# Int8 fake-quantisation in two passes over the data instead of three

## The reference

```python
def _qdq(x):
    s = jnp.maximum(jnp.max(jnp.abs(x), axis=-1, keepdims=True) / 127.0, 1e-08)
    return jnp.clip(jnp.round(x / s), -127.0, 127.0) * s

def _L1_xattn_ref(x, cond, wq, bq, wkv, bkv, wp, bp):     # x: layernorm of the residual
    q = _qdq(x) @ _qdq(wq).T + bq
    kv = cond @ wkv.T + bkv
    ...
    attn = jax.nn.softmax(jnp.einsum('bnhd,bmhd->bhnm', q, k) * scale, axis=-1)   # 16 heads of 16
    o = jnp.einsum('bhnm,bmhd->bnhd', attn, v).reshape(B, N, C)
    out = _qdq(o) @ _qdq(wp).T + bp
    return out
```

## Time and profile before

| | |
|---|---|
| Time, median of 3 executions | 794.25 us (792.49 to 796.47) |
| The profiled execution, its own time | 794.42 us |
| Its span in the profile | 792.6 us |
| TensorE matmul busy | 638.2 us, 81% of the span |
| VectorE busy | 490.2 us, 62% |
| ScalarE busy | 314.7 us, 40% |
| GpSimd busy | 241.4 us, 30% |

### The profile page before, as it was taken

One profiled execution on the slowest core, in us unless ns is written; L12 is line 12 of the kernel. 1 busy time (PEld: TensorE's weight loads), 2 busy tenths in 40 slices (PEclk: granted clock), 3 DMA queues, 4 the chain that ended last, 5 costly groups with the idle time before them and its releaser, 6 DMA issues.

```text
span 792.6 us, 11112 instructions
## 1 busy us (share of the span) xinstructions
PE 638.2 (81%) x3798; PEld 399.0 (50%) x3799; DVE 490.2 (62%) x1022; ACT 314.7 (40%) x534; POOL 241.4 (30%) x247
## 2 busy tenths in 40 slices
PE   1651879986973299999786998887999999999990
PEld 1241525544662135556444666554666666666660
DVE  6998588875988899898666777963222222222223
ACT  4910423324567038887653666502111111111110
POOL 3312055547821199740322312002111111111100
PEclk9675879998996559999987999979999999999996
DMA  7000402010004434651306004970000000000005
GB/s 266 0 0 15 158 0 68 14 54 1 1 1 98 107 91 104 183 152 60 103 7 279 1 1 168 412 310 27 24 24 27 26 26 26 26 22 25 20 15 172
DMA packets 32318, 61.72 MB, mean 78 GB/s; under 512 B 6232, under 2 KB 26712, under 8 KB 29944
## 3 DMA queue, kind: packets, MB, share of 16 engines
q1 hardware_dynamic: 24480, 48.93, 19.3%
q10 hardware_dynamic: 5632, 6.29, 2.2%
q0 software_dynamic: 2160, 5.90, 2.2%
HBM read 47.22 MB, written 13.50 MB: 77 GB/s over the span
## 4 chain that ended last, share of the span: by engine, by line
PE 54%; DVE 32%; issue 6%; POOL 3%; ACT 3%; DMA 2%; SPq 0%; DVEq 0%; POOLq 0%; ACTq 0%
PE bank L1907 18%; PE bank L1928 8%; PE bank L1485 4%; DVE region L1213 3%; PE bank L1126 2%; PE bank L1086 2%; PE bank L1918 2%; DVE XN L366 2%; PE bank L542 2%; PE bank L1110 2%; PE bank L570 2%; PE bank L1505 2%; PE bank L506 2%; DVE region L2217 2%; POOL rstd L380 1%
## 5 line engine op out<-in xcount | busy, mean ns | idle before, releaser
L1907 PE MATMUL bank<-region,wide 128*128 x368 | 142.3, 540 | 1.6 <-issue 1.6
L1786 DVE TENSOR_TENSOR wide<-wide,bank 128x448 f32<-128x448 f32 x46 | 28.5, 621 | 120.0 <-ACT wide L1834 120.0
L1907 PEld LDWEIGHTS bank<-region,wide 128*128 128x128 f32 x368 | 68.1, 190 | 61.7 <-issue 61.5
L1213 DVE TENSOR_REDUCE region<-bank 128x2 f32<-128x512 f32 x128 | 80.1, 680 | 6.9 <-PE bank L1086 6.3
L1684 POOL DMA_INDIRECT choice_results<-wide,to_row x23 | 22.7, 987 | 182.9 <-DVE wide L1799 182.9
L1928 PE MATMUL bank<-region,XN 128*128 x322 | 73.4, 379 | 1.2 <-DVE wide L1799 1.2
L1149 ACT ACTIVATE region<-bank 128x1024 f32<-128x1024 f32 x64 | 62.9, 1024 | 15.6 <-PE bank L1110 15.5
L1834 ACT ACTIVATE wide<-bank 128x448 f32<-128x448 f32 x46 | 24.9, 543 | 106.2 <-PE bank L1907 106.2
L1928 PEld LDWEIGHTS bank<-region,XN 128*128 128x128 f32 x322 | 59.5, 190 | 9.3 <-issue 2.2
L1086 PE MATMUL bank<-region 128*128 128x256 bf16 x256 | 51.9, 304 | 8.8 <-DVE region L1213 6.0
L380 POOL TENSOR_TENSOR rstd<-vareps,half_neg 128x4 f32<-128x4 f32 x16 | 18.3, 1146 | 122.0 <-DVE vareps L376 122.0
(11 more groups left out here) (309 smaller groups left out, 1236.0 us busy)
## 6 DMA issues: line engine op xcount, KB each, us to landing
region<-in_L_ffn_experts_dram SPq DMA_DIRECT2D x8, 2688.0 KB, 15.9
region<-ctx_parts SPq DMA_DIRECT2D x24, 192.0 KB
region<-norm_parts SPq DMA_DIRECT2D x24, 192.0 KB
channel_values<-wide ACTq DMA_DIRECT2D x8, 512.0 KB, 3.8
ctx_parts<-region SPq DMA_DIRECT2D x40, 64.0 KB, 2.0
region<-in_L_ffn_w_gate_up_dram SPq DMA_DIRECT2D x4, 512.0 KB, 6.1
wide<-channel_values SPq DMA_DIRECT2D x16, 128.0 KB, 2.5
norm_parts<-region SPq DMA_DIRECT2D x24, 64.0 KB, 3.6
```

The costliest lines, as they stand in the source:

```text
L1213: e.tensor_reduce(nmax[i % 2][:, at_:at_ + KC], score_bank("scores", n).rearrange("p (c n) -> p c n", c=KC), AX.X, ALU.max, negate=True).t ...
L1786: e.tensor_tensor(HB8[par][:, cols], silu8[:, cols], bank[hf][:, 512:512 + I8 // 2], ALU.mult)\
L1907: last = e.matmul(bank[hf][:, 512 * gu:512 * gu + hw], xbT[par][:, P * c:P * c + P], region[:, bass.ds(off + (2 * gu + c) * I8 + hw * hf, ...
```

## The change

In each of the three places the minimum with 127 and the maximum with -127 are dropped. The first pass now multiplies by the reciprocal and adds `MAGIC`; the second pass is gone; the third is as it was. Nothing is moved, and no wait is added.

```diff
         def quantise(e, ch, src, dst, sc):
...
-            ch.link(e.tensor_scalar(dst, src, sc[:, 2:3], 127.0, ALU.mult, ALU.min))
-            ch.link(e.tensor_scalar(dst, dst, -127.0, MAGIC, ALU.max, ALU.add))
+            ch.link(e.tensor_scalar(dst, src, sc[:, 2:3], MAGIC, ALU.mult, ALU.add))
             return e.tensor_scalar(dst, dst, MAGIC, sc[:, 1:2], ALU.subtract, ALU.mult)
 
         def quantise_in_psum(e, ch, src, dst, sc):
...
-            ch.link(e.tensor_scalar(src, src, sc[:, 2:3], 127.0, ALU.mult, ALU.min))
-            ch.link(e.tensor_scalar(src, src, -127.0, MAGIC, ALU.max, ALU.add))
+            ch.link(e.tensor_scalar(src, src, sc[:, 2:3], MAGIC, ALU.mult, ALU.add))
             return e.tensor_scalar(dst.rearrange("p (h d) -> p h d", d=HD), src, MAGIC, sc[:, 1:2], ALU.subtract, ALU.mult)
...
                 for i in range(lo, hi):
                     xi = XN[:, D * i:D * i + D]
-                    last = e.tensor_scalar(xi, xi, inv[:, i - lo:i - lo + 1], 127.0, ALU.mult, ALU.min)
+                    last = e.tensor_scalar(xi, xi, inv[:, i - lo:i - lo + 1], MAGIC, ALU.mult, ALU.add)
                 ch.link(last)
-                ch.link(e.tensor_scalar(half, half, -127.0, MAGIC, ALU.max, ALU.add))
```

## The result

The changed kernel takes **788.47 us** in the median of 6 runs (787.08 to 790.22). The kernel before took 793.69 us in the median of 6 (792.13 to 796.47). The ratio is 0.9938, with a 95% interval from 0.992 to 0.9955: 5 us less, between 3.6 and 6.3. Forecast were 789.0 us.

The account below looks back on a forecast made before the run. VectorE was taken to bound the edited stretches, except where it waits for TensorE. 1.33 + 1.46 + 0.1 + 1.88 + 0.47 = 5.24 us off the 794.25 us median gave 789.0 us, range 786.5 to 792.3.

Parts of the forecast that it names:

- the likeliest case: Whole kernel: the forecast itself, 5.24 us gained, 789.0 us, own range 787.5 to 790.8, chance 0.62.
- The cost of one pass: Removed VectorE passes, start to start: 0.33 us (weights), 0.73 (normalised input), 0.47 (PSUM); surviving first steps stay at 354 and 494 ns.
- cheaper first steps: All 20 surviving first passes: if as cheap as the two-constant form, another 1.2 us would go; kept for the range.
- Weights, 1.33: Four weight pieces: each removal counts in full in VectorE's stream, 0.33 us each, 1.33 us together.
- Normalised input, 1.46: Two halves of the normalised input: both removals count in full, 0.73 us each, 1.46 us together.
- the cover: TensorE's transposes after the first half: they waited 0.99 us for L729, so their own work ends before its new end.
- The loop, 0.1 + 1.88 + 0 + 0.47: Attention loop, eight tiles: first gives 0.1 us, tiles 1 to 4 give 1.88, 5 and 6 nothing, 7 gives 0.47.
- All the signs: Loop: L769 every 4.91 us, L570 waiting about 0.17, first L769 about 0.4, L786 waits grown to 1.4 and 1.9.
- The rival of the passing on: Loop: it passes to another engine, middle removals become TensorE waits, 3.36 us gained, 790.9 us; chance 0.12.
- Everything counts: All removals reach the end: 6.55 us, or 7.7 with less costly first passes, 787.7 or 786.5 us; chance 0.08.
- Slower: Loop: earlier restart leaves TensorE's clock at half for two and a half rounds, 799.3 us; chance 0.04.
- The clock case: TensorE restarts: half clock lasts longer at two of them, net gain only 2.2 us, 792.0 us; chance 0.14.

Follow-up runs that it names:

- twin: The kernel before once more under another name, without an edit, against the kernel before: 792.13 us (12 runs) beside 792.71, ratio 1.0.
- two_more: The kernel before with two more VectorE passes in each tile of the attention output, against the kernel before: 801.77 us beside 794.24, ratio 1.0085.
- four_more: The kernel before with four more VectorE passes in each attention-output tile, against the kernel before, measured twice: 808.24 us (ratio 1.0193) and 808.64 us (ratio 1.0171).

## Why the prediction was right

**The size.** Forecast 789.0, measured 788.47, within the range and the likeliest case's own. The sum, 5.24 us, stands beside 5.09 us in steps of the trace and 5 us in the medians, which alone could not tell it from 4 or 6.

**The cost of one pass.** Right. The surviving first passes stayed at 354 and 493 ns, so the extra 1.2 us of cheaper first steps did not come. Start to start, a removal gave 0.33, 0.73 and 0.47 us.

**Weights, 1.33.** 1.21 measured, twice. The term was over by 0.12: "all of 1.33 us" took the four as alike, but in the second weight L2209 starts 0.15 us after the end of L391, where the gap in before had been some 0.03. The profile names L391 as what it waited for. That can't be all, since the same pair in the fourth weight has a gap of 0.04 (L391 at 47.13, L2209 at 47.52). The cause wasn't tried and stays open.

**Normalised input, 1.46.** Measured 0.73 and 0.73, and 0.73 and 0.74 in the single edit. TensorE's remaining wait of 0.27 us shows how close the cover was: 0.99 - 0.73 = 0.26.

**The loop, 0.1 + 1.88 + 0 + 0.47.** Measured 0.10, 1.85 and 0.47, with nothing for tiles 5 and 6. All the signs came: rounds of 4.91, L571 waiting 0.17, waits of 1.42 and 1.92. Only the first L769 waited 0.29 and not 0.4, while its shift was the forecast 0.10.

**The rival of the passing on** falls: VectorE is still full, and the kernel with one tile's scale puts TensorE's round at 4.66, where the prediction had 4.74. **Everything counts** falls by the tiles 0, 5 and 6 put back (0.09 us in the trace, not 1.41) and by four passes added for nothing. **Slower** falls: the loop ran at full clock in after.

**The clock case** is half right. There is no price of 4 us for this edit. But the size of the clock's effect in single executions was understated. The prediction used the Trainium skill, "TensorE: Matmul & The Clock Gate", Part 1: The HAM clock gate, for a gate whose window is free-running, and said that the moment of the rise is luck in each run. The traces agree that it is luck: without any edit, twin's shift moved by -1.8, +0.7, +1.6 and -1.7 us at four places. The prediction took before's one profile as the base and stood near the medians, because its 794.42 lay near the median of its own runs; that was luck, and the pair of profiles alone would have given 6.5 us. The prediction also passed over two waits of VectorE for TensorE that lie between an edit and the end, 8.3 us at L737 (93 us) and 4.3 at L769 (191 us, both in before). The gains came through both, because TensorE's work there starts from VectorE's, but these are the places where the clock gave 1.0 and took 0.85 us. The two waits in before:

```profile
...
93.44 0.29 DVE L737 TENSOR_REDUCE region<-bank 128x8 f32<-128x128 f32 x1 [8.30 <-PE bank L495]
...
190.83 1.23 DVE L769 TENSOR_REDUCE region<-bank 128x16 f32<-128x1024 f32 x1 [4.30 <-PE bank L542]
...
```

**What stays open.** The single edit in PSUM measured 3.7 us where its trace shows 2.4. Four added passes measured 15.3 and 13.6 us where the loop shows 12.8 in both traces. If dips of the clock get rarer as rounds get shorter, a part of the gain could be clock after all. In the profiles, a dip in the loop's last rounds stands in 2 of 5 with rounds of 5.38 us, where it cost 1.6 us each time, in 0 of 5 with shorter rounds and in 3 of 3 with longer ones. That fits, but thirteen profiles are few, and the whole change's 5 us leave no room for more than about a microsecond of it. The other way, behind TensorE's restart at 185 us the five profiles with the edit at the normalised input were at half clock for 5.0 us in the mean and the eight without it for 4.5. That may be luck, or a price of some 0.3 us for the earlier restart.

## What to carry to other kernels

Price a removed instruction start to start in its own stream, then ask tile by tile who waits at that place. The first and last rounds of a pipelined loop have other limits than the middle: 3 of 8 equal removals here were worth 0.1 us together, and four passes added in the same place cost nothing. For edits of a microsecond, pair the instructions of two traces and read the steps of the shift, since single steps of 0.1 us stand out clearly where medians of 12 runs scatter by a microsecond. Then hold each step against the granted clock of the two stretches before calling it the edit's. An engine with a long wait ahead of it in the chain is worth a look at the order of its queue: moving one root gave over half of what fourteen removed passes gave.

## What the runs showed of the hardware that was not expected

**Half clock in a busy loop.** TensorE's clock fell to half inside a loop that kept it busy. In two_more it was busy 12.33 us of the 15 from 197 to 212, all at full clock, before a first fall of 3.4 us, and 9.59 of the 13 from 216 to 229, all at full, before a second one of 6.8 us. In four_more it was busy 19.46 of 29 us, all at full clock, before it fell. In twin, with rounds of 5.38 us, it was busy 28.41 of 33 us at full before it fell. In after, with rounds of 4.91 us, it was busy 30.69 of 32.6 and did not fall. What decides it is not settled: before, with twin's rounds, did not fall either.

**Two engines on one memory.** The scan L2211 took 2.27 us while GpSimd ran L2026 beside it, and 1.20 us when the products were moved away, all else equal; so moving the root gave more than the 2.06 us of its wait. The Trainium skill, "SBUF — State Buffer", section "SBUF: two separate sides", says that VectorE with two inputs in this memory and GpSimd share one pair of ports, which one of them holds for a whole instruction. The trace agrees roughly: L2026 ends at 63.12 + 1.26 = 64.38, a scan of 1.20 us from there would end at 65.58, and it ended at 63.19 + 2.27 = 65.46.
